# Graph attention, feed-forward and expert mixture on one core: the go of an edge pass waited for at its beginning, statistics and clears moved, the output matrix split in quarters

## The reference, cut to what matters

```python
x = x + gnn0(layernorm(x), edges)   # 4 heads of attention over the edges, skip, Wlin, layer norm with gamma, beta
x = x + ffn0(layernorm(x))          # 4 experts with a threshold gate, low-rank lora_A, lora_B, then fc2
x = x + gnn1(layernorm(x), edges, edge_attr)   # mean of the edge attributes, W1, relu, W2
x = x + ffn1(layernorm(x))          # self-attention (8 heads, output matrix Wo), norm, argmax expert of 8, norm
```

## Time and profile before

| | |
|---|---|
| three runs | 1892.71, 1898.34 (median), 1900.72 us |
| the profiled execution | 1899.85 us, span 1898.2 us |
| mean granted TensorE clock | 0.972 |
| PE busy | 1765.4 us, 93% of the span |
| DVE, ACT, POOL busy | 1307.2, 913.3, 591.2 us (69%, 48%, 31%) |

### The profile page before, as it was taken

How to read it: one execution, slowest core, us unless ns; L and a number is a source line. 1 busy time by engine, 2 the same in 40 slices (tenths; PEclk the granted TensorE clock), 3 DMA queues, 4 the chain that set the end, 5 groups by cost and what they waited for, 6 DMA issues and landing times. The chain is left out here.

```text
span 1898.2 us, 31991 instructions
## 1 busy us (share of the span) xinstructions
PE 1765.4 (93%) x10970; PEld 1537.4 (81%) x10970; DVE 1307.2 (69%) x2964; ACT 913.3 (48%) x1660; POOL 591.2 (31%) x532
## 2 busy tenths in 40 slices
PE   7998999799999999999689999999899999999596
PEld 5776899688888888788578998988688888888585
DVE  6444466688888888377665565545588787887776
ACT  4332266577777776222331243324465555555421
POOL 0000102555556552011101212222254545444344
PEclk9999999899999999999899999999899999999798
DMA  7652677877777775667222049875020202112632
GB/s 246 213 196 77 203 240 250 221 200 204 201 204 198 203 204 142 156 169 186 86 78 73 1 131 162 203 207 182 11 44 1 66 7 58 32 32 71 217 123 89
DMA packets 183532, 265.14 MB, mean 140 GB/s; under 512 B 55852, under 2 KB 102443, under 8 KB 181109
## 3 DMA queue, kind: packets, MB, share of 16 engines
q1 hardware_dynamic: 117839, 169.58, 30.9%
q0 software_dynamic: 49920, 62.94, 12.4%
q10 hardware_dynamic: 15640, 30.90, 6.6%
HBM read 198.55 MB, written 85.86 MB: 150 GB/s over the span
## 5 line engine op out<-in xcount | busy, mean ns | idle before, releaser
L1103 POOL DMA_INDIRECT edge_rows<-xn_store,edge_index x200 | 242.4, 1212 | 173.5 <-PE psum L138 112.3
L2616 POOL TENSOR_TENSOR mprob<-mprob,mrden 125x1250 f32<-125x1250 f32 x80 | 181.6, 2271 | 222.2 <-DVE mrden L2730 221.7
L2645 ACT ACTIVATE mprob<-psum,mbias 125x1250 f32<-125x1250 f32 x80 | 104.3, 1303 | 154.5 <-DVE mbias L2739 154.5
L1321 DVE TENSOR_TENSOR edge_xt_lo<-psum,edge_xt_hi 128x500 fp32r<-128x500 f32 x200 | 134.8, 675 | 59.3 <-ACT edge_xt_hi L1196 59.3
L1196 ACT ACTIVATE edge_xt_hi<-psum 128x500 fp32r<-128x500 f32 x200 | 117.6, 589 | 94.5 <-PE psum L1497 94.5
L2737 DVE TENSOR_REDUCE mmin<-psum 125x1 f32<-125x512 f32 (+1 forms) x240 | 127.0, 584 | 47.4 <-PE psum L2919 47.2
L2937 PE MATMUL psum<-ident,mprob 125*125 125x125 f32 x800 | 117.2, 291 | 17.5 <-DVE ptm_lo L2744 9.4
L2937 PEld LDWEIGHTS psum<-ident,mprob 125*125 125x125 f32 x800 | 99.7, 190 | 35.1 <-DVE ptm_lo L2744 20.4
L2744 DVE TENSOR_TENSOR ptm_lo<-psum,ptm_hi 125x500 fp32r<-125x500 f32 (+1 forms) x240 | 126.4, 582 | 2.0 <-ACT ptm_hi L2651 2.0
L1497 PE MATMUL psum<-ident,edge_rows 125*128 125x125 f32 x800 | 120.2, 273 | 7.6 <-POOLq L1110 5.1
L1350 DVE TENSOR_TENSOR edge_rows_lo<-edge_rows,edge_rows_hi 125x1024 fp32r<-125x1024 f32 x100 | 121.2, 1212 | 0.0
(11 more groups left out here) (530 smaller groups left out, 5355.3 us busy)
## 6 DMA issues: line engine op xcount, KB each, us to landing
slots_in<-blank_rows ACTq DMA_DIRECT2D x20, 1026.0 KB, 16.5
t_store<-t_part SPq DMA_DIRECT2D x20, 1000.0 KB, 5.3
t_row<-t_store SPq DMA_DIRECT2D x47, 400.0 KB, 6.7
y_store<-y_rows SPq DMA_DIRECT2D x50, 200.0 KB
q_chunk<-q_store SPq DMA_DIRECT2D x40, 250.0 KB, 5.3
y_tile<-y_store SPq DMA_DIRECT2D x10, 896.0 KB
edge_attr<-in_attr SPq DMA_DIRECT2D x50, 112.0 KB
moe_xg<-slots_in SPq DMA_DIRECT2D x17, 256.5 KB, 3.0
```

Of the source, the lines that this page charges most:

```text
L1103: nc.gpsimd.indirect_dma_start(xe[t % RING][:, s, :], None, g.xn_store, bass.IndirectOffsetOnAxis(ap=index[t % RING][:, s, 0:1], axis=0)). ...
L1321: nc.vector.tensor_tensor(xt_lo[:, k, :], x_bank(KT * t + k), f32(xt_hi[:, k, :]), ALU.subtract).then_inc(x_low, 1)
L2616: nc.gpsimd.tensor_tensor(prob[:, n % 4, :], prob[:, n % 4, :], rden[:, n % 4:n % 4 + 1].broadcast_to([P, N]), ALU.mult).then_inc(p_ready, 1)
```

## The change

- The waits for `pass_go` on POOL, ACT, DVE and PE move from the end of a turn to its beginning; SP gives the first go itself, behind its read of `passes`. POOL adds to `pass_over` at the beginning.
- SP's 18 clears of `turn_inner` move ahead of the last store and get a wait for the last edge sums (`agg_done`).
- Steps 14 and 15 of the fourth pair (tiles 6 and 7) leave the pass; in `dense_stages` DVE does them behind its four normal rows, and ACT makes rows 6 and 7 later, behind a new semaphore.
- The split of the output matrix is done in four pieces of 128 x 512, ACT at n = 5 to 8, DVE at n = 6 to 9.

```diff
@@ SP, graph_attention
             passes = sp.value_load(g.passes_i[0:1, 0:1], min_val=1, max_val=2 * ROUNDS - 1)
+            sp.sem_inc(pass_go, 1)
             with sp.Fori(0, passes) as turn:
...
+                sp.wait_ge(agg_done, WINDOWS)
+                for s in turn_inner:
+                    sp.sem_clear(s)
                 sp.wait_ge(o_added, NT)
                 in_two(sp, pair(g.base_store, FIN), g.acc[:, 2 * FIN:, :], base_out)
-                for s in turn_inner:
-                    sp.sem_clear(s)
                 sp.wait_ge(pass_done, 4 * turn + 4)
@@ POOL
             with pool.Fori(0, passes) as turn:
+                pool.wait_ge(pass_go, turn + 1)
+                pool.sem_inc(pass_over, 1)
                 for t in range(RING):
                     index_load(pool, t, first_index_in)
...
                 pool.sem_inc(pass_done, 1)
-                pool.wait_ge(pass_go, turn + 1)
@@ ACT (DVE and PE alike)
             with act.Fori(0, passes) as turn:
+                act.wait_ge(pass_go, turn + 1)
...
-                act.wait_ge(pass_go, turn + 1)
@@ DVE, finish(c, step)
-                if step == 14:
+                if step == 14 and c < FIN - 1:
                     dve.wait_ge(xin_used, 2 * c + 2)
                     fin.spread(nc, link, c, g.acc)
                     fin.moments(nc, link, c)
-                if step == 15:
+                if step == 15 and c < FIN - 1:
                     link(fin.scale(nc, link, c))
@@ ACT, dense_stages
-            for t in range(4, 8):
+            def late_row(t):
                 nc.scalar.activation(xs[:, t, :], g.acc[:, t, :], ACT.Identity, bias=fin.shift2[:, t:t + 1],
                                      scale=fin.r2[:, t:t + 1]).then_inc(late_xs, 1)
+            for t in range(4, 6):
+                late_row(t)
             for t in range(2):
                 first_hi(t)
             for t in range(4):
                 copy_x(t)
             for t in range(2, 6):
                 first_hi(t)
+            act.wait_ge(late_scale, 1)
+            for t in range(6, 8):
+                late_row(t)
@@ DVE, dense_stages
             for t in range(4):
                 first_normal_row(t)
-            for t in range(6):
+            fin.spread(nc, link, last_pair - 1, g.acc)
+            first_lo(0), first_lo(1)
+            fin.moments(nc, link, last_pair - 1)
+            fin.scale(nc, link, last_pair - 1).then_inc(late_scale, 1)
+            for t in range(2, 6):
                 first_lo(t)
@@ self_attention: SP, ACT, DVE, PE
-            sp.wait_ge(wo_ready, 1)
+            sp.wait_ge(wo_ready, KT)
...
-                    if n == 4 and isinstance(c, int) and c == 0:
+                    if 5 <= n < 5 + KT and isinstance(c, int) and c == 0:
                         act.wait_ge(g.wo_in, 16)
-                        nc.scalar.activation(wo_hi[:], raw[:], ACT.Copy).then_inc(wo_h, 1)
+                        nc.scalar.activation(wo_hi[:, n - 5, :], raw[:, n - 5, :], ACT.Copy).then_inc(wo_h, 1)
...
-                    if n == 4 and isinstance(c, int) and c == 0:
-                        dve.wait_ge(wo_h, 1)
-                        nc.vector.tensor_tensor(wo_lo[:], raw[:], f32(wo_hi[:]), ALU.subtract).then_inc(wo_ready, 1)
+                    if 6 <= n < 6 + KT and isinstance(c, int) and c == 0:
+                        k = n - 6
+                        dve.wait_ge(wo_h, k + 1)
+                        nc.vector.tensor_tensor(wo_lo[:, k, :], raw[:, k, :], f32(wo_hi[:, k, :]), ALU.subtract).then_inc(wo_ready, 1)
...
-                pe.wait_ge(wo_ready, 1)
+                pe.wait_ge(wo_ready, KT)
```

More of the change, by code:

```diff
@@ L1423, in _ @@
             with dve.Fori(0, passes) as turn:
+                dve.wait_ge(pass_go, turn + 1)
                 others(0)
@@ L1464, in _ @@
                 g.pass_flags(nc).then_inc(pass_done, 1)
-                dve.wait_ge(pass_go, turn + 1)
         @block.tensor
@@ L1569, in _ @@
             with pe.Fori(0, passes) as turn:
+                pe.wait_ge(pass_go, turn + 1)
                 for k in range(KT):
@@ L1590, in _ @@
                 pe.sem_inc(pass_done, 1)
-                pe.wait_ge(pass_go, turn + 1)
 TILES = (N + 8 * 127) // 128
@@ L1678, in dense_stages @@
     raw_free = [sem("ffn_raw_free0"), sem("ffn_raw_free1")]
+    late_scale = sem("ffn_late_scale")
     all_xs, late_xs, x_copied, fin_done = sem("ffn_xs"), sem("ffn_late_xs"), sem("ffn_x_copied"), sem("fin_done")
@@ L2114, in add_out @@
                 nc.vector.tensor_tensor(x[:, n % NT, :], x[:, n % NT, :], core.bank(s)[0:P, :], ALU.add).then_inc(added, 1)
+            last_pair = NC - 1
             for t in range(4):
                 first_normal_row(t)
-            for t in range(6):
+            fin.spread(nc, link, last_pair - 1, g.acc)
[3 more added lines that the diff above has]
+            for t in range(2, 6):
                 first_lo(t)
-            last_pair = NC - 1
             for c in range(NC):
```

## The result

| | before | changed |
|---|---|---|
| median of the runs | 1899.05 us (4 runs) | 1913.56 us (4 runs, 1910.47 to 1915.35) |
| profiled execution, its span | 1899.85, 1898.2 us | 1915.35, 1913.5 us |
| ratio to before, 95% interval | | 1.0080 (1.0061 to 1.0099) |
| mean granted TensorE clock | 0.972 | 0.965 |

The account below looks back on a forecast made before the run. PE, busy 93% of the span, was taken as the bound, so edits count only where it stands or is made to stand. 21.8 - 6.6 + 1.1 - 3.1 = +13.2 us on 1898.3 gave 1911.5 us; 8-in-10 range 1904 to 1919.5.

Parts of the forecast that it names:

- First go: Edge pass entry: POOL's index loads and gathers start 28.1 us later, shorter landings give some back; +21.8 us.
- Pass end: End of the edge pass: 4.2 us of DVE statistics and 2.4 us of POOL's drain leave PE's wait; -6.6 us.
- Clears: End of the pass: SP's 18 clears cost nothing on the path before or after their move; zero.
- Beginning of the next block: Moved statistics on DVE and ACT's later rows 6 and 7 delay `fc_hi`; +1.1 us, between 0 and 2.5.
- Output matrix: Self-attention: splitting in quarters takes DVE's block and its wait off PE's path; -3.1 us, between -2 and -3.5.
- Quiet queues: Rival, pass entry: index loads and gathers land so fast that PE's floor of 17.7 holds; +9.1, 1907.4 us; chance 0.17.
- No landing is shortened: Rival, pass entry: no transfer lands sooner, so all 28.1 us stay; +19.5, 1917.8 us; chance 0.10.
- the drain stays: Rival, pass end: POOL's drain begins only at the block's real end, only 4.2 us come off; +15.6, 1913.9 us; chance 0.10.
- the go comes early: Rival, pass entry: SP's go reaches POOL before its stores are issued, POOL starts as before; -8.6, 1889.7 us; chance 0.03.

Follow-up runs that it names:

- experiment 11: The kernel before run once more, unaltered, for a second trace: 1899.2 us, ratio 1.0009.
- experiment 3: Kernel before with the waits at the beginning and SP's first go at the very beginning of its share; rest unchanged: 1895.84 us, ratio 0.9983.
- experiment 6: Kernel before with only the fourth pair's statistics moved from the pass to the next block: 1896.22 us, ratio 0.9978.
- experiment 9: Changed kernel with SP's first go at the head of its share and without the move of the fourth pair's statistics: 1893.22 us, ratio 0.9976.
- experiment 4: Changed kernel, late first go kept for ACT, DVE and PE, but POOL waits at the end of its turn: 1889.04 us, ratio 0.9956.
- experiment 1: Changed kernel with SP's first go moved to the beginning of its share, ahead of every store: 1888.39 us, ratio 0.9956; second set 1894.7 us, 0.9952.

## Why the prediction was right

**Forecast 1911.5 us, slower; measured 1913.56.** The side and the mechanism were right. Its steps in order:

- *First go, +21.8.* The mechanism is right. The entry takes 67.4 us late (mean of three) and 45.9 early (mean of ten): +21.5; by the runs 22.8. Against the one trace that I read, though, it is 19.8 (67.29 to 47.52), and there the terms were off. From the first index load to the first gather the time fell from 11.95 us (309.50 to 321.45) to 8.25, so 3.7 came back in place of 2.0; from the first gather to the ninth it fell from 21.29 to 16.93, 4.4 in place of 2.9; window 2's last gather took 7.6 us in place of 7.9, so 0.3 in place of 1.4. Together 8.4 against 6.3. POOL's first index load came 30.8 us later, 2.4 of which are PE's parts, which ended that much later in this trace: 28.4 against 28.1. So some 20 us where I had 21.8. The forecast fits the mean because the trace that I read has one of the long early entries (experiment 11): that is luck. First turns at 359.06 and window 2 at 377.75 fit; the stand was 23.87 us, not over 25.
- *Pass end, -6.6.* Right: 15.24 to 8.42 is 6.8; experiments 3 and 6 give the halves, 2.4 for the drain and 4.2 to 4.3 for the statistics.
- *Clears, 0.* Right.
- *Beginning of the next block, +1.1.* The piece is 0.86, and the upper bound of 2.5 was too low for what followed. I took everything behind `hid_lo` as unchanged. It is not: to the gates' rows the changed kernel takes 47.1 to 47.2 us against 43.5 to 45.7 in the kernel before and its variants without the move, 3.0 us more in the mean (47.18 of five traces, 44.18 of seven), and the rows show the clock as the difference. It falls behind waits of PE that are hardly longer than before (experiment 9). That is the term that was missing.
- *Output matrix, -3.1.* Under-sized: 4.7 us by the runs and by the traces (14.7 to 10.0 for the two steps), outside my -3.5, though the runs' interval of 2.5 to 7.2 takes it in. In the trace that I read the two steps took 13.09 us, which gives just the 3.1. The step of 8.66 us in the trace I read is 9.57 or 9.58 in five others, and the step behind it took 4.80 to 5.86 us there at a granted clock of 0.65 to 0.92, in place of 4.43 us at 1.00 in the trace I read.

Corrected: 21.5 - 6.8 + 0.9 + 3.0 - 4.7 = +13.9; measured +14.5 and +13.5 (0.0071 of 1898.45). The two errors, +3.0 and -1.6, partly offset each other, and the entry came out right only through the trace that I happened to read; so the closeness of 1911.5 was in part luck.

**The rivals.** *Quiet queues* (+9.1) was nearer than I gave it credit for in the landings: 4.3 to 4.5 us for most of window 1's gathers. The entry stayed at +21.5 and not 17.7, because the ninth gather still waited 5.06 us and PE 5.35 us before window 2. The Trainium skill (DMA: Bandwidth & Descriptors, "Anatomy of one DMA — SWDGE (gpsimd) path") puts a fixed 2.0 us and bytes over 436 GB/s on such a transfer, from which I estimate 2.6 us for 256 KB. That lies under every landing of a gather that these traces show, 3.9 us at the least. *No landing is shortened* is refuted by the rows of the landings, *the drain stays* by experiments 3 and 4, and *the go comes early* is what experiment 1 had to build. The Trainium skill (VectorE: DVE Perf Modes, "The DRAIN you can't avoid") gives about 12 ns on all five engines for the boilerplate drains at a program's beginning and end. POOL's drain at the end of this block took 2685 to 2690 ns in the fourteen traces, wherever it stands; whether it is of the kind that the Trainium skill means, no run shows.

## What to carry to other kernels

A wait that moves from the end of a loop to its beginning is passed once more, at the very start, and what counts there is where in its giver's queue the first signal stands: here behind the stores of the parts, 28 us after POOL came to the pass, and in front of a chain of transfers that had been hidden. Give such a first signal at the head of the giver's list, and look for the engine with the longest lead (POOL here), not for the one that does the work. By their ratios the parts alone were worth 3.2 + 4.2 + 4.7 + 1.3 = 13.4 us (waits with the early go, statistics, matrix, clears), all together 8.4 to 9.1. The intervals of the single parts are 2 to 3 us to either side each, so this doesn't show whether such gains add up; of the 1.3 us of the clears the traces show nothing.

A term read from one trace can be that execution's. The entry and the matrix steps of the trace read here lay 1.6 us from the mean of their kind. A second trace of the same kernel, cut at the same places, shows which terms are steady.

## What the runs showed of the hardware

- POOL's drain at the end of this block took 2685 to 2690 ns in every trace, whether it came right behind work or behind a wait for SP. ACT's and PE's took 8 and 13 ns behind a wait (five traces), and 1004 to 1006 and 2468 to 2508 ns where the engine came straight from its work (nine). Moving a wait away from the end of a block puts all of these beside other engines' work.
- The same matmuls behind waits of the same length ran at either clock level: behind PE's waits of 2.2 to 2.9 us on the way to the gates the next 4 us were granted 1.00 or 0.50 to 0.64, in one kernel 0.60 in one trace and 1.00 in the other (behind `hid_lo`). How often it was low went with the kernel. In the five traces with the moved statistics and a stand of 8.4 us the stretch to the gates ran at 0.87 in the mean, a mixture of both levels, 1.2 and 2.4 GHz. With the moved statistics and a stand of 10.9 us it was 0.89 and 0.93 (experiments 4 and 6), and without the move, with stands of 12.6 to 15.2 us, 0.93 to 1.00 (seven traces). Whether the shorter stand or the new order of DVE's and ACT's work behind it does this is open; no run changed the one alone over the whole way, and the kernels without the move differ among themselves at nearly the same stand (15.0 to 15.2 us: 43.5 to 45.7).
- The Trainium skill (TensorE: Matmul & The Clock Gate, "Part 1: The HAM clock gate (the "warmup" mystery)") says that how many matmuls run slow varies from run to run of one kernel. The traces agree: the kernel before took 44.32 us for this stretch at a granted clock of 0.96, and 43.53 at 1.00 when it ran again.
